# Wider pair sums, high parts and first key/value steps on ScalarE, and a three-step prefix in an attention and expert kernel

## The reference, cut to what matters

```
xn   = batch norm of x;  q, k, v = qkv_w @ xn + qkv_b           # 4 heads of 32 channels
attn = softmax(q . k / sqrt(128)) over the 1024 keys;  x = x + out_w @ (attn @ v) + out_b
t    = tokens of x
u    = layer norm of t;  k', v' = per-head norms of u with weights and biases (8 heads of 16)
t    = t + u + u @ (k'^T v' / N) per head                       # 16 x 16 product per head
z2   = layer norm of t;  probs = softmax(z2 @ gate_w + gate_b) over 8 experts
t    = t + sum over the two best experts e of probs[e] * (gelu(z2 @ W1[e] + b1[e]) @ W2[e] + b2[e])
```

## Time and profile before

| what | value |
|---|---|
| median of 3 executions | 2252.08 us (2238.56 to 2256.55) |
| profiled execution | 2246.34 us, its span 2244.6 us |
| TensorE (PE) busy | 1754.7 us, 78% of the span |
| weight loads (PEld) | 884.2 us, 39% |
| VectorE (DVE) busy | 1379.7 us, 61% |
| ScalarE (ACT) busy | 1071.3 us, 48% |
| GpSimd (POOL) busy | 1434.8 us, 64% |
| mean granted TensorE clock | 0.863 of full speed |

### The profile page before, as it was taken

One profiled execution on the slowest core, in us unless ns is written; L12 is line 12 of the kernel. 1 busy time (PEld: TensorE's weight loads), 2 busy tenths in 40 slices (PEclk: granted clock), 3 DMA queues, 4 the chain that ended last, 5 costly groups with the idle time before them and its releaser, 6 DMA issues.

```text
span 2244.6 us, 38139 instructions
## 1 busy us (share of the span) xinstructions
PE 1754.7 (78%) x11103; PEld 884.2 (39%) x11256; DVE 1379.7 (61%) x3701; ACT 1071.3 (48%) x1898; POOL 1434.8 (64%) x1779
## 2 busy tenths in 40 slices
PE   5999898897888989798898978885337677777744
PEld 2233333332333333333333333333326566566632
DVE  5677878686776768677686866754434333333345
ACT  1565655555455555545455555452115444444432
POOL 1777587875968678596877769676335555555530
PEclk8999999998988999799898999896568888887865
DMA  2220220211202022120202112010323333322259
GB/s 64 57 57 12 55 81 17 76 37 51 77 14 84 15 76 53 38 77 21 76 13 75 47 44 73 6 38 31 101 76 119 107 115 96 93 76 75 74 150 319
DMA packets 130824, 155.20 MB, mean 69 GB/s; under 512 B 19678, under 2 KB 93170, under 8 KB 130688
## 3 DMA queue, kind: packets, MB, share of 16 engines
q1 hardware_dynamic: 113408, 117.76, 18.9%
q0 software_dynamic: 16896, 35.69, 4.7%
q10 hardware_dynamic: 384, 0.00, 0.0%
HBM read 65.03 MB, written 55.84 MB: 54 GB/s over the span
## 4 chain that ended last, share of the span: by engine, by line
PE 49%; issue 14%; DVE 12%; another core or an unknown queue 8%; POOL 6%; ACT 5%; SPq 4%; DMA 1%; DVEq 0%; ACTq 0%; POOLq 0%
PE psum L1573 8%; PE psum L1620 7%; PE psum L1593 7%; PE psum L1683 6%; DVE rowmax L1198 5%; PE psum L1670 5%; PE psum L1554 3%; PE psum L1421 3%; POOL probs L624 2%; PE psum L1428 2%; PE psum L1576 2%; PE psum L1659 2%; PE psum L1458 1%; POOL arena L624 1%
## 5 line engine op out<-in xcount | busy, mean ns | idle before, releaser
L1198 DVE TENSOR_REDUCE rowmax<-psum 128x1 f32<-128x512 f32 x1024 | 670.1, 681 | 304.3 <-PE psum L1620 184.9
L1620 PE MATMUL psum<-arena 128*128 128x512 bf16 x872 | 332.9, 405 | 103.8 <-DVE rowmax L1198 81.1
L797 ACT ACTIVATE probs<-psum 128x1024 f32<-128x1024 f32 x256 | 251.1, 1021 | 209.7 <-PE psum L1576 203.5
L797 ACT ACTIVATE arena<-psum 128x1024 f32<-128x1024 f32 x256 | 252.7, 1021 | 179.8 <-PE psum L1576 176.6
L610 POOL DMA_INDIRECT sorted_scratch<-rows,slot_idx x256 | 251.1, 981 | 91.9 <-issue 69.6
L1620 PEld LDWEIGHTS psum<-arena 128*128 128x128 bf16 x1024 | 92.5, 101 | 550.0 <-DVE rowmax L1198 384.9
L1573 PE MATMUL psum<-qk 32*128 32x512 f32 x2048 | 300.6, 657 | 7.9 <-ACT probs L797 4.3
L1683 PE MATMUL psum<-probs 128*128 x1088 | 186.4, 326 | 100.5 <-ACT probs L866 100.4
L624 POOL TENSOR_TENSOR probs<-probs 128x256 f32<-128x256 f32 x352 | 243.7, 729 | 16.5 <-PE psum L1593 13.5
L624 POOL TENSOR_TENSOR arena<-arena 128x256 f32<-128x256 f32 x352 | 243.9, 728 | 13.5 <-PE psum L1593 10.9
L1683 PEld LDWEIGHTS psum<-probs 128*128 128x128 f32 x1088 | 174.9, 236 | 128.9 <-issue 121.6
(11 more groups left out here) (203 smaller groups left out, 2794.3 us busy)
## 6 DMA issues: line engine op xcount, KB each, us to landing
arena<-part SPq DMA_DIRECT2D x256, 128.0 KB, 2.8
qk<-sorted_scratch SPq DMA_DIRECT2D x136, 144.0 KB
probs<-y_scratch SPq DMA_DIRECT2D x64, 256.0 KB, 5.1
x_in<-in_x_dram SPq DMA_DIRECT2D x16, 512.0 KB, 3.5
x_res<-in_x_dram SPq DMA_DIRECT2D x16, 512.0 KB
t_scratch<-t SPq DMA_DIRECT2D x16, 512.0 KB
arena<-t_scratch SPq DMA_DIRECT2D x8, 1024.0 KB
out_dram<-probs SPq DMA_DIRECT2D x32, 256.0 KB, 5.3
```

The source lines that it names most:

```text
L797: a.activation(group[:, 2 * i:2 * i + 2, :].rearrange("p s n -> p (s n)"), st_pair[i], ACT.Exp, scale=float(C) ** -0.5).then_inc(exp_done, 1)
L1198: v.tensor_reduce(rowmax[:, half, kh, h, j:j + 1], ps[:, :], AX.X, ALU.max)\
L1620: t_.matmul(ps[:, :], qs1[:, par, h, qb * P:(qb + 1) * P], ks1[:, par, h, kh * HALF:(kh + 1) * HALF], start=True, stop=True)\
```

## The change

It has five parts. (1) `SUM_PARTS` goes from 8 to 4, so that a pair sum is four instructions of 512 columns. (2) The bf16 high part of queries and keys is written by ScalarE from PSUM, just ahead of its raw copy; POOL keeps only the subtraction, and ScalarE waits at q0 for the transfers of the image before, which read the same `part`. In the startup VectorE's two casts go the same way. (3) The four steps behind gram are ScalarE's; the head mask is multiplied into the value weights once at setup, so `kv_product` has one step less. (4) The prefix is three additions of 64 columns (neighbours, then distance two, then four) with zero blocks ahead of them; two pairs of slot operations become one instruction each. (5) The table has new places: zT1 27 to 24, z (19, 19, 20, 20) to (19, 19, 19, 20), ss 25 to 23, prefix (27, 28, 31).

```diff
-    PAIRS, SUM_PARTS = 4, 8
+    PAIRS, SUM_PARTS = 4, 4
...
                 pool.wait_ge(raw_ready, 4 * b + c + 1)
-                g.tensor_copy(part[:, 0, which, cols], qk[:, par, which, cols]).then_inc(high_ready, 1)
-                pool.wait_ge(high_ready, parts_made(b, c))
+                pool.wait_ge(high_ready, 4 * b + c + 1)
                 g.tensor_tensor(part[:, 1, which, cols], qk[:, par, which, cols], part[:, 0, which, cols],
                                 ALU.subtract).then_inc(mid_ready, 1)
...
+                    if b > 0 and name == "q0":
+
+                        for h in range(NH):
+                            act.wait_ge(stacked1[1 - par][h], 16 * STACK1_DMAS * ((b - 1) // 2 + 1))
+                    a.activation(part[:, 0, which, cols], ps[:, :], ACT.Identity,
+                                 bias=bqk[:, which:which + 1]).then_inc(high_ready, 1)
                     a.activation(qk[:, par, which, cols], ps[:, :], ACT.Identity,
                                  bias=bqk[:, which:which + 1]).then_inc(raw_ready, 1)
...
+                elif name == "gram":
+                    ps = from_shared(name, pair, p)
+                    a.activation(usum[:, :], ps[:, C:C + 1], ACT.Copy).then_inc(gram_out, 1)
+                    a.activation(kvw[:, 0, :], ps[:, 0:C], ACT.Copy, scale=kcol[:, 0:1]).then_inc(gram_out, 1)
+                    act.wait_ge(gram_out, 3 * b + 1)
+                    a.activation(udiag[:, :], ident[:, :], ACT.Copy, scale=usum[:, :]).then_inc(udiag_ready, 1)
+                    a.activation(kcc[:, :], usum[:, :], ACT.Identity, scale=kcol[:, 0:1], bias=kb_n[:, :])\
+                     .then_inc(gram_out, 1)
...
-            v.memset(before[:, 0, :], 0.0).then_inc(dve_const, 1)
+            for t in (before[:, 0:1, :], chosen[:, 0:1, :], two_of[:, 0:2, :], four_of[:, 0:4, :]):
+                v.memset(t, 0.0).then_inc(zeros_in, 1)
+            dve.wait_ge(zeros_in, 4)
...
+                for j in range(2):
+                    v.tensor_tensor(vrow[:, j, :], vrow[:, j, :], headmask[:, :], ALU.mult).then_inc(dve_const, 1)
...
-                if name == "gram":
-                    ps = from_shared(name, pair, p)
-                    v.tensor_copy(usum[:, :], ps[:, C:C + 1]).then_inc(kv_step, 1)
-                    dve.wait_ge(kv_step, 6 * b + 1)
-                    v.tensor_scalar(udiag[:, :], ident[:, :], usum[:, :], None, ALU.mult).then_inc(udiag_ready, 1)
-                    v.tensor_scalar(kvw[:, 0, :], ps[:, 0:C], kcol[:, 0:1], None, ALU.mult).then_inc(kv_step, 1)
-                    v.scalar_tensor_tensor(kcc[:, :], usum[:, :], kcol[:, 0:1], kb_n[:, :], ALU.mult, ALU.add)\
-                     .then_inc(kv_step, 1)
...
-                    v.tensor_tensor(kvw[:, 4, :], kvw[:, 3, :], headmask[:, :], ALU.mult).then_inc(bd_ready, 1)
-                    dve.wait_ge(bd_ready, 2 * b + 1)
-                    v.tensor_tensor(bd[:, :], kvw[:, 4, :], ident[:, :], ALU.add).then_inc(bd_ready, 1)
-
+                    dve.wait_ge(kv_step, 3 * b + 3)
+                    v.tensor_tensor(bd[:, :], kvw[:, 2, :], kvw[:, 3, :], ALU.add).then_inc(bd_ready, 1)
...
+                for k in steps:
                     if k == 0:
                         dve.wait_ge(gate_step, 16 * b + 15)
+                        ins = v.tensor_tensor(two_of[:, 2:, :], chosen[:, 1:, :], chosen[:, 0:BLK, :], ALU.add)
+                    elif k == 1:
+                        dve.wait_ge(prefix_step, 3 * b + 1)
+                        ins = v.tensor_tensor(four_of[:, 4:, :], two_of[:, 2:, :], two_of[:, 0:BLK, :], ALU.add)
                     else:
-                        dve.wait_ge(prefix_step, 8 * b + k)
-                    v.tensor_tensor(before[:, k + 1, :], before[:, k, :], lg[:, 8, k, :], ALU.add)\
-                     .then_inc(prefix_step, 1)
+                        dve.wait_ge(prefix_step, 3 * b + 2)
+                        ins = v.tensor_tensor(before[:, 1:, :], four_of[:, 4:, :], four_of[:, 0:BLK, :], ALU.add)
+                    ins.then_inc(prefix_step, 1)
...
-                for c in range(2):
-                    v.tensor_tensor(slot[:, 1 + c, :, :], slot[:, 0, :, :], lg[:, 6 + c, :, :], ALU.mult)\
-                     .then_inc(slot_step, 1)
+                v.tensor_tensor(slot[:, 1:3, :, :], slot[:, 0:1, :, :].broadcast_to([P, 2, BLK, E]), lg[:, 6:8, :, :],
+                                ALU.mult).then_inc(slot_step, 1)
...
-                for c in range(2):
-                    v.tensor_reduce(slot_of[:, c, :], slot[:, 1 + c, :, :], AX.X, ALU.add).then_inc(slot_step, 1)
-                dve.wait_ge(slot_step, 6 * b + 6)
+                v.tensor_reduce(slot_of[:, :, :], slot[:, 1:3, :, :], AX.X, ALU.add).then_inc(slot_step, 1)
+                dve.wait_ge(slot_step, 4 * b + 4)
```

More of the change, by code:

```diff
@@ L80, in conv_attention_hybrid_kernel @@
     out_v = out.rearrange("b c h w -> b c (h w)")
-    AT = {'q0': 2, 'k0': 3, 'q1': 4, 'k1': 7, 'rank': 1, 't2_0': 8, 't2_1': 10, 'proj0': 11, 'proj1': 12, 'mrow1': 13, 'v0': 14, 'v1': 15, 'z2T0': 17, 'z2T1': 18, 'logits': 19, 'zT0': 23, 'zT1': 27, 'mrow0': 29, 'gram': 28, 'usum': 30, 'xn': 1, 'values1': 0, 'values0': 17, 'x_bias': 27, 'ln1': 10, 'z2': (12, 14, 15, 17), 'gexp': 20, 'ln0': 16, 'z': (19, 19, 20, 20), 'square': 22, 'ln_heads': 26, 'split': (2, 3, 5, 6), 'norm1': 6, 'norm0': 30, 'd16': 20, 'u': 23, 'scatter': (9, 11, 12, 14, 17, 17, 20, 24), 'max1': 12, 'max0': 28, 'kv1': 2, 'kv2': 4, 'kv3': 4, 'slot_numbers': 2, 'stats1a': 8, 'stats1b': 10, 'deviations1': 11, 'gate': (20, 23, 23, 23, 24, 24, 24, 24, 25, 25, 26, 26, 26, 26, 27, 29), 'prefix': (27, 27, 27, 27, 28, 28, 30, 31), 'stats0a': 11, 'stats0b': 12, 'deviations0': 17, 'gsum': 20, 'ss': 25, 'heads': 26, 'turn': 1, 'den_sum': 2, 'sum': (5, 9, 13, 19), 'den1': 5, 'den0': 21}
+    AT = {'q0': 2, 'k0': 3, 'q1': 4, 'k1': 7, 'rank': 1, 't2_0': 8, 't2_1': 10, 'proj0': 11, 'proj1': 12, 'mrow1': 13, 'v0': 14, 'v1': 15, 'z2T0': 17, 'z2T1': 18, 'logits': 19, 'zT0': 23, 'zT1': 24, 'mrow0': 29, 'gram': 28, 'usum': 30, 'xn': 1, 'values1': 0, 'values0': 17, 'x_bias': 27, 'ln1': 10, 'z2': (12, 14, 15, 17), 'gexp': 20, 'ln0': 16, 'z': (19, 19, 19, 20), 'square': 22, 'ln_heads': 26, 'split': (2, 3, 5, 6), 'norm1': 6, 'norm0': 30, 'd16': 20, 'u': 23, 'scatter': (9, 11, 12, 14, 17, 17, 20, 24), 'max1': 12, 'max0': 28, 'kv1': 2, 'kv2': 4, 'kv3': 4, 'slot_numbers': 2, 'stats1a': 8, 'stats1b': 10, 'deviations1': 11, 'gate': (20, 23, 23, 23, 24, 24, 24, 24, 25, 25, 26, 26, 26, 26, 27, 29), 'prefix': (27, 28, 31), 'stats0a': 11, 'stats0b': 12, 'deviations0': 17, 'gsum': 20, 'ss': 23, 'heads': 26, 'turn': 1, 'den_sum': 2, 'sum': (5, 9, 13, 19), 'den1': 5, 'den0': 21}
     LAG = {
@@ L253, in conv_attention_hybrid_kernel @@
         before = sb("before", [P, BLK + 1, E])
+        chosen = sb("chosen", [P, 1 + BLK, E])
+        two_of = sb("two_of", [P, 2 + BLK, E])
+        four_of = sb("four_of", [P, 4 + BLK, E])
         slot = sb("slot", [P, 3, BLK, E])
@@ L1236, in iteration @@
                         gate(b, p, [i for i in range(16) if AT["gate"][i] == q])
-                        prefix(b, [k for k in range(BLK) if AT["prefix"][k] == q])
+                        prefix(b, [k for k in range(3) if AT["prefix"][k] == q])
                     if in_range(-1, pair, p):
```

56 lines of the change are left out of this document (28 added, 28 removed).

## The result

The changed kernel takes 2361.3 us, the median of four runs (2350.0 to 2367.4); the kernel before, beside it, 2246.8. The ratio is 1.050 (95% interval 1.044 to 1.057): the change makes it 5% slower, 115 us, and the forecast of 2236 us (2202 to 2268) was wrong. In what follows DVE is VectorE and POOL is GpSimd.

The account below looks back on a forecast made before the run. Up to about 1600 us TensorE is 87% busy and no side engine full, so TensorE's waits for them count. Terms +10 + 4.5 - 19.5 - 6 - 4 - 1 = -16 us gave 2236 us as median, range 2202 to 2268.

Parts of the forecast that it names:

- Part 1: Pair sums in 512 columns: VectorE's longer waits in quarters 17 to 19 cost +10 us, ends -8 and +20.
- the 3.66 us row: VectorE standard-deviation step in quarters 17 to 19 while POOL adds; priced as ending 0.6 us earlier, in 4 images.
- Part 4: Three prefix additions for eight, mostly quarters 27 and 28, and merged slot operations: 0 on the path.
- Part 2: High parts by ScalarE: second copy delays denominators, +4.5 us; earlier transfers shorten the mrow1 wait, -19.5 us (0 to -32).
- only moves stalls: Third rival, within the forecast's 0.49: all terms but Part 2 and Part 3 give nothing; 2250 us.
- Part 3: Steps after gram on ScalarE: scores start 0.4 us earlier in 15 images, -6 us, ends -10 and +15.
- The other terms (-4 and -1): Six z blocks in quarter 19 bring the burst forward, -4 us (0 to -10); drained end and setup, -1 (±3).
- VectorE is blocked longer: Rival, chance 0.15: longer POOL instructions hold VectorE's two-source steps, +36 from quarters 17 to 19, +5 gram's exp; 2285 us.
- POOL's lateness is the real bound: Rival, chance 0.36: both "remote" waits end with POOL's scatter runs, which come earlier; -50 us, 2202 us.

Follow-up runs that it names:

- e3: The changed kernel with the sums back in 256 columns (eight pieces, not four): 2208.7 us, 0.989 of the kernel before.
- e4: The kernel before with only the sums changed, four of 512 columns in place of eight of 256: 2379.5 us, 1.068.
- m1: Not the model: 67 trials of one small VectorE step issued into a GpSimd run of sums, most 67 ns later each time; longest step at most 1.32 us.
- m3: Not the model: the small VectorE step issued 3 ns later per trial into sums of 512, 256, 128 and 341 columns, 84 trials; at most 1.32 us.
- e10: The kernel before, 256-column sums, with only the three-step prefix of the change: 2234.9 us, 0.996.
- e1: The changed kernel with the second prefix step issued in quarter 27, not 28: 2335.3 us, 1.044.
- e2: The changed kernel with the old prefix in eight steps at their old places, 512-column sums kept: 2377.4 us, 1.063.
- e9: The changed kernel with 256-column sums and the high parts taken off ScalarE again (GpSimd copies them): 0.992 of the kernel before.
- e8: The changed kernel with 256-column sums and the four steps behind gram on VectorE again: 1.003 of the kernel before.
- e3_again: Repeat of e3 (changed kernel, 256-column sums) on another chip: 0.996 of the kernel before.
- e15: The changed kernel, 512-column sums kept, with a one-column memset and a GpSimd wait for it behind each scatter: 2135.3 us, 0.953.
- e5: The changed kernel, 512-column sums kept, with GpSimd waiting behind each sum until it has ended: 2226.8 us, 0.996.
- m4: Not the model: 61 trials of the small VectorE step, with or without indirect transfers ahead of the sums; 512 columns: 9.7 to 10.8 us right behind, otherwise at most 1.2.
- e7: The changed kernel with the sums in six pieces of 341 or 342 columns: 2335.8 us, 1.043 of the kernel before.
- e6: The changed kernel with sums of 128 columns, sixteen per pair: 2382.4 us, 1.065.
- m2: Not the model: the small VectorE step issued 99 ns later per trial into sums, with signals, ScalarE or TensorE busy, singly and together; at most 1.32 us.

## Why the prediction was wrong, step by step

**Part 1, the step that failed.** The sum had +10 us for VectorE's longer waits, with ends at -8 and +20; the width costs 122 to 137 us (1.0502 over e3's 0.9959 and 0.9891), and 153 in e4. Two readings failed in it, besides the 6.2 us an image for the sums, which measured 4.6. It took one sum per step as the unit and looked for blocked steps in quarters 17 to 19 alone; there the 1.2 us came as forecast. And it noted that the 3.66 us row spans five POOL instructions and does not agree with the lock that the Trainium skill describes (SBUF — State Buffer, Who interferes with whom), then priced that row as a harmless form, "0.6 us earlier". That row was the change's loss in small. The two images of the earlier trace rows differ in what stood ahead of POOL's burst, and the earlier trace rows itself shows it for one of them, 1.26 us of idle time at 1014.65. For the other the timeline of the kernel before has:

```profile
911.83 0.97 POOL L610 DMA_INDIRECT sorted_scratch<-rows,slot_idx  x1 [0.30 <-issue]
912.81 5.50 POOL L624 TENSOR_TENSOR probs<-probs 128x256 f32<-128x256 f32 x8
```

The burst follows the transfer without a pause, and the step at 914.69 is held to its end. The lock itself is borne out in m1 to m3, where no transfer stands ahead: the two-source additions wait for the end of the sum that they meet, 1.32 us at most, and end 0.12 us behind the start of the next.

**Part 4, "0 on the path".** True at 256 columns (e10). At 512 the step it put into quarter 28 is the one that waits 10.6 us. But e1 and e2 show that this place was not the cause: take that step away, and the next one with two sources in SBUF is passed over.

**Part 2** (-15 in all: +4.5 and -19.5). The copy of mrow1 should have followed its matmul by 4.4 us; it follows by 1.4, but the wait stands one projection earlier at 3.37 us. The e9 pair can't tell a gain from none: -15 is not confirmed, and the third rival's "only moves stalls" describes the trace better. No run took the transfers alone away, so what the "remote" waits are for stays open.

**Part 3** (-6). Scores start 2.0 us after gram's last result (1128.50 to 1130.49), 2.3 were forecast and 2.7 stood before. The right direction, sized small: at 256 columns e8 says 15, about 8 either way. The other terms (-4 and -1) were not tried by themselves. All terms but part 1 add up to -26 us; with the width undone the change gained 9 (e3_again) to 24 us (e3).

**The rivals.** "VectorE is blocked longer" (0.15, 2285 us; its own terms, 2252 + 41 - 4, add up to 2289) named the right pair of engines and the right sign, but its place was quarters 17 to 19, its unit again one sum, and its price about a third. "POOL's lateness is the real bound" (0.36, 2202 us) is closer to what the kernel does once the long waits are gone, and e15, at 0.953, lies below even it. "It only moves stalls" counts parts 2 and 3 alone, which give 2231 us and not its 2250. No case held both the long waits and what lies behind them.

## What to carry to other kernels

An instruction that takes many times its usual duration is a finding, not noise: ask which instructions of the other engine it spans and what stood ahead of those, before giving it a price. When a shorter queue on GpSimd is the aim, look at what the change does behind its indirect transfers: a one-column memset and a wait for it there turned a 5% loss into a 5% gain. Pauses elsewhere cost time: with one behind every sum (e5) the kernel was at 0.996. And where one blocked step is moved away and the time stays, the cause is on the side of the one that blocks.

## What the runs showed of the hardware

- Behind an indirect transfer, an unbroken run of GpSimd's sums kept a VectorE step out to its end, 9.7 to 11.4 us in 25 of 25 trials at 512, 341 and 128 columns (m4). With 0.09 us of idle time ahead of the run (e15: the memset ends at 1082.36, the run begins at 1082.45), or a wait for the transfer (m4), it waited for one sum. A memset without a wait for it, as m4 has between transfer and run, does not help. Why a transfer has this effect no run shows.
- At 256 columns it did so in none of 8 trials and in 9 of the 67 waiting steps behind a transfer in the kernel before (15 of 51 in e10, 12 of 65 in e9). No run shows why; other widths but 512, 341 and 128 were not tried behind a transfer.
- Without a transfer ahead no step was passed over in the 242 trials, nor in the changed kernel, e1 and e7; in e6 (128 columns) 20 of 41 were, and in e3 (256) 9 of 93, these for one more sum (0.76 to 0.77 us in all). No run shows why.
- ScalarE and TensorE, both busy beside it, changed nothing in m2. A copy from SBUF to SBUF waited like a step with two sources (m1); row maxima, read from PSUM, never did (0.70 us at most in the changed kernel and in e15).
